# Attention plus experts on one core: a value tile kept twice, paired value products, expert outputs gathered in sorted order

## The chip, the cores and the metric

The kernel runs on one core of a Trainium2 chip. The metric is the device time of that core in microseconds (us). Differences of about 0.5% (6.5 us) are what a measurement of this kernel can tell from none.

## The reference

The input is x, 8 batches of 512 tokens with 256 channels, all float32. Layer norm, causal attention with 16 heads of 16 channels (rotary embedding on queries and keys), output projection, residual; then layer norm, a router that picks 2 of 8 experts for each token, a gated expert, and a residual again:

```
q, k, v = heads(norm(x) @ W.T + b);  q, k = rope(q), rope(k)
attn = softmax(where(causal, q @ k.T / 4, -inf));  x = x + heads_back(attn @ v) @ Wo.T + bo
logits = norm(x) @ router_w + router_b;  top 2 experts per token, probs = softmax(top 2 logits)
# each expert takes cap = int(1.2 * 2 * 512 / 8) = 153 rows of each batch, 8 * 153 = 1224 rows in all
h = rows @ w_c_fc + b_c_fc;  g = rows @ w_gate + b_gate        # 256 -> 1024
o = silu(h * g) @ w_c_proj + b_c_proj                          # 1024 -> 256
x = x + probs[0] * o[expert 0, pos 0] + probs[1] * o[expert 1, pos 1]
```

## The kernel before

Every engine has a program of its own, written out by hand; semaphores join them. There is no planner: the order of the work is the order in the code.

**Attention phase.** body(b) is one batch on each engine; it has 4 groups g of 4 heads, and each group has 8 slots u. A slot scores one block of 128 queries for two heads (pass 1, line 438, its row maxima taken by VectorE at line 823) and one block of 128 keys for two heads of the group two steps back (pass 2, lines 450 and 456, its exponentials taken by ScalarE at lines 599 and 607 into the tile probs). Between the slots TensorE does "pieces" for neighbouring batches, by the table PIECES: M transposes the row maxima (line 486), A the attention outputs of a finished group, X the normalised rows, Q and V are projections, T and O the output projection, H, L, R and F the router. free_banks makes TensorE wait, before slot u, for the maxima of slot u-2 (red_done) and the exponentials of slot u-2. The piece M in slot 0 waits for all eight maxima of the group before it. Batches 2 to 6 are one hardware loop (Fori) on each of the five engines; 0, 1, 7 and 8 are written out.

The value path: VectorE adds the bias to the value projection (line 804) into v_next, in slots (2, 5) and (3, 6) of the batch before. In slot (2, 1), with all products of the batch before done, it copies v_next (line 828) into v_sb, whose heads are padded from 16 to 32 columns, the padding holding ones. The product pv (line 467) has the values as its weights, 32 columns wide, one head at each multiple of 32 output rows, and the probabilities as the moving operand: for key block j it is 4 heads in two passes, 8 records of 512 - 128j columns. pv for j = 0, 1, 2 stands in slots 3, 5, 7, and j = 3 in slot 1 of the next group. probs holds two key blocks, so the exponentials of block j wait for the products of block j-2. Afterwards ScalarE copies the whole bank of sums (line 623) in slot 2, and piece A transposes it in slot 3.

**Expert phase.** Each expert has three blocks n of 384, 384 and 456 rows, and each block has 8 chunks hc of 128 hidden channels. For a chunk TensorE makes the fc and the gate products (line 77) in two PSUM banks each; ScalarE adds a bias to fc (line 1389), VectorE multiplies (gated, line 1484), ScalarE applies silu (line 1378), VectorE rounds to ah (line 1437), and GpSimd subtracts to al (line 1520); in the last expert VectorE does that from chunk (1, 1) on (line 1446). The output projection of a block (10 tiles of up to 128 rows per expert, 24 products each) stands after chunk 2 of the next block; VectorE adds the bias (tiles_out, line 1471) and SP stores the tile (line 1239). TensorE's gate product of chunk u needs the gated product of chunk u-2, and a projection tile needs the tile two before it put out. GpSimd also splits the weights of the next expert.

**The end.** Each token needs two rows of the expert outputs. GpSimd gathers them by indirect DMA (line 1573), 128 rows each, 8 per batch and 64 in all, in the order of the router's choices, so that a batch's rows can be those of the last expert. A batch is gathered when the last expert's tiles that hold its rows are stored. VectorE multiplies and adds (combine, line 1456, 8 per batch) to the rows loaded back into y by ScalarE's queue (line 1409), and that queue stores the result (line 1417). The loads and all sums come after the last projection.

```
            def combine(b):
                dve.wait_ge(gathered[b % len(got)], 16 * NB * (b // len(got) + 1))
                dve.wait_ge(ld_y[b % 4], 16 * (b // 4 + 1))
```

## Time and profile before

| | |
|---|---|
| runs | 1305.95, 1298.87, 1300.56 us; median 1300.56 |
| the profiled execution | 1304.85 us, of which the profile's span is 1303.0 us |
| busy in the span | TensorE 91%, VectorE 56%, ScalarE 37%, GpSimd 53% |
| TensorE busy, attention, 150 to 250 us | 94.8% |
| TensorE busy, experts, 800 to 1000 us | 99.7% |
| last 53 us | TensorE 9.6 us busy, GpSimd 34.6, VectorE 28.1 |
| chain that ended last | TensorE 48% of the span, GpSimd 2%, DMA and VectorE under 1% |
| mean granted clock of TensorE | 0.96 of full speed |

The time of an execution is its span and about 2 us around it. A "busy" matmul is a pipelined one, so busy shares near 95% still hide small losses; the starts of the instructions tell more. The attention phase ends near 560 us, the experts run to 1259 us, and what follows is gathering and adding.

### The profile page before, as it was taken

What the parts mean: (1) busy time and instruction counts of PE and PEld (TensorE: products, weight loads), DVE (VectorE), ACT (ScalarE), POOL (GpSimd) and SP (SyncE); (2) the same over time, 40 slices, a digit from 0 to 9 for tenths busy, and PEclk for the clock granted to TensorE, in tenths of its full rate; (3) what the DMA queues carried; (4) which work ended last, traced back from release to release, by engine and by line L of the source; (5) the groups of instructions that cost most, each with busy time, mean ns of one, the idle gap of its engine ahead of it and who ended that gap; (6) DMA issues with size and microseconds to landing.
All of it is one profiled execution on the core that took longest, in us unless ns stands there. A gap on an engine that the chain in (4) does not pass through costs nothing.

```text
span 1303.0 us, 25602 instructions
## 1 busy us (share of the span) xinstructions
PE 1181.2 (91%) x8264; PEld 1007.5 (77%) x8264; DVE 733.7 (56%) x1512; ACT 482.5 (37%) x988; POOL 696.3 (53%) x984
## 2 busy tenths in 40 slices
PE   3699999999999999878999999999999999999950
PEld 3466666665656576578899999999999999999950
DVE  5777787878787877755343333343433333333554
ACT  2155454545454545533333323333222333322310
POOL 4334335353535343577567655576655666742675
PEclk9699999999999999979999999999999999999985
DMA  4876745454545454442221122221111312101366
GB/s 132 213 243 178 228 115 161 113 160 113 160 113 160 113 145 113 143 136 86 74 66 58 57 75 75 74 82 57 66 63 66 109 58 66 57 29 37 102 207 235
DMA packets 83101, 147.86 MB, mean 113 GB/s; under 512 B 9647, under 2 KB 60728, under 8 KB 78910
## 3 DMA queue, kind: packets, MB, share of 16 engines
q1 hardware_dynamic: 65344, 111.37, 29.8%
q0 software_dynamic: 7936, 26.60, 6.0%
q10 hardware_dynamic: 9728, 8.67, 2.1%
q8 instruction: 56, 0.92, 0.3%
q14 instruction: 37, 0.30, 0.1%
HBM read 93.05 MB, written 53.61 MB: 113 GB/s over the span
## 4 chain that ended last, share of the span: by engine, by line
PE 48%; POOL 2%; issue 1%; DVE 0%; DMA 0%; POOLq 0%; ACT 0%; DVEq 0%
PE ps L77 47%; PE ps L1293 1%; POOL wf_hi L1573 1%; POOL wg_hi L1573 1%; POOL wp_lo L1573 0%; DVE raw L1456 0%; DMA wg_hi<-slot_outputs,slot_all 0%; DMA slot_outputs<-o_sb 0%; POOLq L1601 0%; DVE al L1446 0%; DVE xl L1361 0%; POOL wg_lo L1573 0%; DVE ah L1437 0%; ACT fc L1389 0%; POOLq L1573 0%
## 5 line engine op out<-in xcount | busy, mean ns | idle before, releaser
L1520 POOL TENSOR_TENSOR al<-hid,ah 128x384 fp32r<-128x384 f32 (+1 forms) x176 | 187.4, 1065 | 234.4 <-DVE ah L1437 234.4
L1389 ACT ACTIVATE fc<-ps,b_fc 128x384 f32<-128x384 f32 (+1 forms) x192 | 115.6, 602 | 453.2 <-PE ps L77 453.2
L1484 DVE SCALAR_TENSOR_TENSOR gated<-ps,b_gate,fc 128x384 f32<-128x384 f32 (+1 forms) x192 | 123.4, 643 | 238.8 <-PE ps L77 223.2
L823 DVE TENSOR_REDUCE mx<-ps 128x2 f32<-128x256 f32 (+3 forms) x256 | 206.1, 819 | 34.2 <-PE ps L438 31.6
L438 PE MATMUL ps<-kst,qst 65*128 65x256 f32 (+2 forms) x512 | 149.5, 375 | 10.7 <-DMA kst<-qk_parts 10.7
L607 ACT ACTIVATE probs<-ps 128x512 f32<-128x512 f32 (+1 forms) x256 | 122.9, 538 | 60.0 <-PE ps L456 59.5
L1471 DVE TENSOR_TENSOR o_sb<-ps,b_proj 128x256 f32<-128x256 f32 x80 | 33.9, 424 | 175.8 <-PE ps L77 175.8
L599 ACT ACTIVATE probs<-ps 128x256 f32<-128x256 f32 (+1 forms) x128 | 62.6, 490 | 144.3 <-PE ps L450 144.0
L964 POOL TENSOR_TENSOR rope_c<-qk_b,rope_table 128x512 f32<-128x512 f32 x32 | 43.5, 1358 | 118.4 <-ACT qk_b L635 118.3
L77 PE MATMUL ps<-xh,wg_hi 128*128 128x384 f32 (+1 forms) x384 | 103.7, 351 | 0.0
L77 PE MATMUL ps<-xh,wg_lo 128*128 128x384 f32 (+1 forms) x384 | 103.4, 351 | 0.0
L77 PE MATMUL ps<-xl,wg_hi 128*128 128x384 f32 (+1 forms) x384 | 103.4, 350 | 0.0
L1378 ACT ACTIVATE hid<-gated 128x384 f32<-128x384 f32 (+1 forms) x192 | 102.8, 535 | 1.3 <-DVE gated L1484 1.3
L467 PE MATMUL ps<-probs,v_sb 128*32 128x512 f32 (+3 forms) x1024 | 95.5, 444 | 7.5 <-DVE v_sb L828 7.5
L77 PE MATMUL ps<-wp_hi,ah 128*128 128x256 f32 (+1 forms) x640 | 89.4, 282 | 2.8 <-DVE al L1446 2.8
L77 PE MATMUL ps<-xh,wf 128*128 128x384 f32 (+1 forms) x384 | 89.1, 354 | 0.6 <-issue 0.5
L438 PEld LDWEIGHTS ps<-kst,qst 65*128 65x128 f32 x512 | 80.5, 198 | 11.1 <-DMA kst<-qk_parts 10.9
L77 PE MATMUL ps<-wp_hi,al 128*128 128x256 f32 (+1 forms) x640 | 89.0, 281 | 0.0
L1437 DVE CAST ah<-hid 128x384 fp32r<-128x384 f32 (+1 forms) x192 | 88.3, 460 | 0.8 <-ACT hid L1378 0.8
L77 PE MATMUL ps<-wp_lo,ah 128*128 128x256 f32 (+1 forms) x640 | 88.6, 281 | 0.0
L77 PEld LDWEIGHTS ps<-wp_hi,ah 128*128 128x128 f32 (+1 forms) x640 | 83.0, 185 | 3.5 <-issue 3.2
L993 POOL DMA_INDIRECT slot_tokens<-hn,put_at x64 | 63.8, 997 | 37.6 <-DVE put_at L777 21.3
(181 smaller groups left out, 2491.7 us busy)
## 6 DMA issues: line engine op xcount, KB each, us to landing
qk_parts<-hilo SPq DMA_DIRECT2D x32, 512.0 KB, 2.8
qst<-qk_parts SPq DMA_DIRECT2D x64, 256.0 KB, 4.8
kst<-qk_parts SPq DMA_DIRECT2D x64, 256.0 KB, 5.3
slot_tokens<-zeros POOLq DMA_DIRECT2D x12, 816.0 KB, 6.3
rows<-slot_tokens SPq DMA_DIRECT2D x24, 384.0 KB, 3.4
slot_outputs<-o_sb SPq DMA_DIRECT2D x72, 128.0 KB, 1.7
raw<-in_wf SPq DMA_DIRECT2D x8, 1024.0 KB, 5.4
raw<-in_wg SPq DMA_DIRECT2D x8, 1024.0 KB, 7.9
```

The costliest lines, as they stand in the source:

```text
L77: last = nc.tensor.matmul(out, w, x, start=(i == 0), stop=(i == len(terms) - 1))
L438: last = mm(bank, qst[0:MROW, g, h, bass.ts(i, P)], kst[0:MROW, g, h, 0:width], start=False, stop=True, skip_group_check=True)
L467: last = mm(pvb[32 * h:32 * h + 32, P * j:T], v_sb[:, j, GH * g + h, :], probs[:, j % 2, h, P * j:T], start=(j == 0), stop=(j == TT - 1))
L599: A(probs[:, j % 2, 2 * pr:2 * pr + 2, P * j:T], in_pairs(banks2(u)[0])[:, :, P * j - q0:T - q0], ACT.Exp, scale=float(DH) ** -0.5).then_i ...
L607: A(probs[:, j % 2, 2 * pr + hh, P * j:T], ps[:, banks2(u)[hh], P * j - q0:T - q0], ACT.Exp, scale=float(DH) ** -0.5).then_inc(exp_done, 1)
L823: V.reduce_max(mx[:, g % 2, 2 * pr:2 * pr + 2, i], both[:, :, 0:P * (i + 1)], AXX)\
L993: G.indirect_dma_start(out=rt["tok"], out_offset=bass.IndirectOffsetOnAxis(ap=put_at[:, n:n + 1], axis=0), in_=hn[:, n // K, :], in_offset ...
L1378: A(hid[:, hc % 2, 0:width], gated[:, hc % 2, 0:width], ACT.Silu).then_inc(hid_done, 1)
L1389: A(fc[:, hc % 2, 0:width], ps[:, FC + hc % 2, 0:width], ACT.Identity, bias=b_fc[:, e, hc:hc + 1]).then_inc(fc_out, 1)
L1437: V.tensor_copy(ah[:, (8 * n + hc) % RING, 0:width], hid[:, hc % 2, 0:width]).then_inc(ah_done, 1)
L1484: V.scalar_tensor_tensor(gated[:, hc % 2, 0:width], ps[:, GATE + hc % 2, 0:width], b_gate[:, e, hc:hc + 1], fc[:, hc % 2, 0:width], ALU.ad ...
L1520: G.tensor_tensor(al[:, at, 0:width], hid[:, hc % 2, 0:width], ah[:, at, 0:width].bitcast(F32), ALU.subtract).then_inc(al_done, 1)
```

## The change

- v_sb is two tiles, one for even and one for odd batches, with 17 columns per head; the bias add of the value projection writes it directly. v_next, the copy in slot (2, 1) and its semaphore are gone. The weights of pv are 17 columns wide, still at multiples of 32 output rows. The fill with ones moves from before the last value add of the opening to a place behind the small constants.
- probs is four tiles, one for each key block. pv for j = 0 and 1 both stand in slot 5, and for j = 2 and 3 in slot 1 of the next group. The exponentials of block j wait for the products of the same block of the group before.
- The loop over batches 2 to 6 is written out on all five engines.
- At the first chunk of the last expert VectorE sorts each token's two rows (11 small operations): the lower one always lies in an expert before the last. GpSimd gathers the lower rows of all batches (32 gathers) during the last expert, then the higher ones (32), batch by batch as they are stored. The higher rows use four buffers, the lower ones eight.
- The sums are half as long (4 operations) and 10 of the 16 stand between output tiles of the last two experts; y is loaded by ScalarE's queue from chunks 3 to 6 of the last expert on, and the first two stores follow in its last block.
- VectorE does all 24 subtractions of the last expert.

```
-        v_next = sb("v_next", [P, TT, C])
-        v_sb = sb("v_sb", [P, TT, HEADS, 2 * DH])
+        v_sb = sb("v_sb", [P, 2, TT, HEADS, DH + 1])
-        probs = sb("probs", [P, 2, GH, T])
+        probs = [sb(f"probs{j}", [P, GH, T - P * j]) for j in range(TT)]
...
-                    last = mm(pvb[32 * h:32 * h + 32, P * j:T], v_sb[:, j, GH * g + h, :], probs[:, j % 2, h, P * j:T],
+                    last = mm(pvb[32 * h:32 * h + DH + 1, P * j:T], v_sb[:, bt % 2, j, GH * g + h, :], probs[j][:, h, :],
...
-                        if u in (3, 5, 7) and (not isinstance(b, int) or 0 <= s - 2 <= 31):
-                            pv(s - 2, b - (g < 2), (g - 2) % 4, (u - 3) // 2)
+                        if u == 5 and (not isinstance(b, int) or 0 <= s - 2 <= 31):
+                            pv(s - 2, b - (g < 2), (g - 2) % 4, 0)
+                            pv(s - 2, b - (g < 2), (g - 2) % 4, 1)
                         if u == 1 and (not isinstance(b, int) or 0 <= s - 3 <= 31):
+                            pv(s - 3, b - (g < 3), (g - 3) % 4, 2)
                             pv(s - 3, b - (g < 3), (g - 3) % 4, 3)
...
-            with pe.Fori(2, 7) as b:
+            for b in range(2, 7):
                 body(b)
...
-                        wait(act, pv_done, 4 * t + j - 1)
+                        wait(act, pv_done, 4 * t + j - 3)
...
-                if (g, u) == (2, 1) and there(b, 0, 7):
-                    wait(dve, v_out, 2 * (b + 1))
-                    wait(dve, pv_done, 16 * b)
-                    V.tensor_copy(v_sb[:, :, :, 0:DH],
-                                  v_next[:].rearrange("p t (h r) -> p t h r", h=HEADS)).then_inc(v_moved, 1)
...
+        LOAD_Y_AT = ((0, 3), (0, 4), (0, 5), (0, 6))
+        STORE_Y_AT = ((2, 6), (2, 7))
+        COMBINE_AT = {
+            (LAST - 1, 2, 2): ((0, 0),), (LAST - 1, 2, 3): ((1, 0),),
+            (LAST, 0, 1): ((2, 0),), (LAST, 0, 2): ((3, 0),),
+            (LAST, 1, 1): ((0, 1),), (LAST, 1, 2): ((1, 1),),
+            (LAST, 2, 0): ((2, 1),), (LAST, 2, 1): ((3, 1),), (LAST, 2, 2): ((4, 0),), (LAST, 2, 3): ((5, 0),),
+        }
+        COMBINE_LAST = ((4, 1), (6, 0), (5, 1), (7, 0), (6, 1), (7, 1))
...
+            def combine(b, k):
+
+                if k == 0:
+                    dve.wait_ge(ld_y[b % len(y)], 16 * (b // len(y) + 1))
+                    dve.wait_ge(got_low[b], 16 * TT)
+                else:
+                    dve.wait_ge(low_sum, b + 1)
+                    dve.wait_ge(got_high[b], 16 * TT)
...
             def tiles_out(e, half, n, par):
...
                 for k, size in tiles(n):
+                    for b, kind in COMBINE_AT.get((e, n, k), ()) if isinstance(e, int) else ():
+                        combine(b, kind)
...
+            pool.wait_ge(gate_done, 24 * LAST)
+            pool.wait_ge(sorted_rows, 1)
+            for i in range(OB):
+                pool.wait_ge(st_o[i], 16 * NTE // OB * (LAST - 1))
+            for k in range(2):
+                for b in range(BATCH):
+                    gather(b, k)
```

The keys of COMBINE_AT are (expert, block, tile), its values (batch, 0 for the lower row or 1 for the higher), and the sum stands before that tile is put out.

## Rows read from the trace of the kernel before

**Rows 1.** Waits of TensorE, 60 to 560 us: total us, times, longest us.

```profile
PE ps L467 <- DVE v_sb L828: 7.5, 6, 1.3
PE ps L419 <- DVE mx L823: 6.1, 7, 1.0
```

**Rows 2.** Instructions that write v_sb: duration ns min/median/max, first and last start.

```profile
L828 DVE COPY v_sb<-v_next x8: 678/2528/2534, 70.6 to 507.2; 128x1024 f32<-128x1024 f32 x8
```

**Rows 3.** Timeline around the copy in slot (2, 1): start us, us, instruction [idle before].

```profile
258.37 1.06 PE L467 MATMUL ps<-probs,v_sb 128*32 128x512 f32 x8 [1.27 <-DVE v_sb L828]
...
260.25 1.28 DVE L823 TENSOR_REDUCE mx<-ps 128x2 f32<-128x512 f32 x2
...
261.07 0.28 PE L419 MATMUL ps<-causal_bf,ident_bf 128*128 128x128 bf16 x2 [1.04 <-DVE mx L823]
```

**Rows 4.** Timeline of TensorE, 300 to 345 us: slots with and without a value product.

```profile
306.51 1.07 PE L467 MATMUL ps<-probs,v_sb 128*32 128x512 f32 x8
307.51 0.66 PE L473 MATMUL ps<-consts_sb,pv_sb 128*128 128x128 f32 x4
...
313.14 0.40 PE L450 MATMUL ps<-qst,kst 66*128 66x256 f32 x2
313.38 0.63 PE L77 MATMUL ps<-xnT_hi,wq_hi 128*128 128x512 f32 x2
...
315.46 0.40 PE L450 MATMUL ps<-qst,kst 66*128 66x256 f32 x2
315.79 0.64 PE L467 MATMUL ps<-probs,v_sb 128*32 128x256 f32 x8
316.36 0.28 PE L429 MATMUL ps<-later_bf,ident_bf 128*128 128x128 bf16 x2
```

**Rows 5.** Timeline, the last maxima of a group and the piece M behind them.

```profile
284.05 2.36 DVE L823 TENSOR_REDUCE mx<-ps 128x2 f32<-128x1024 f32 x2
286.63 0.27 PE L486 MATMUL ps<-consts_sb,mx 128*16 128x128 f32 x1
335.51 0.27 PE L486 MATMUL ps<-consts_sb,mx 128*16 128x128 f32 x1 [0.45 <-DVE mx L823]
```

**Rows 6.** Timeline of VectorE in the opening, 0 to 60 us.

```profile
21.02 0.01 DVE L845 LOAD_MASK_SELECT rope_s<-qk_b  x1 [2.69 <-ACT qk_b L635]
...
36.80 1.76 DVE L909 MEMSET v_sb<- 128x2048 f32 x1 [0.38 <-issue]
```

**Rows 7.** Chain that ended last, its stores and landings: start us, us, what.

```profile
1254.42 2.39 DMA slot_outputs<-o_sb
...
1293.36 2.75 DMA wg_hi<-slot_outputs,slot_all
```

**Rows 8.** Line 1573, gathers of two batches: duration ns, first and last start us.

```profile
L1573 POOL DMA_INDIRECT wf_lo<-slot_outputs,slot_all x8: 994/998/1438, 1239.6 to 1249.3; - x8
...
L1573 POOL DMA_INDIRECT wp_lo<-slot_outputs,slot_all x8: 994/1144/1456, 1261.0 to 1271.5; - x8
```

**Rows 9.** Timeline of the end: the last eight sums.

```profile
1296.13 3.38 DVE L1456 SCALAR_TENSOR_TENSOR raw<-wg_hi,prob_all,raw 128x256 f32<-128x256 f32 x8 [5.76 <-DMA wg_hi<-slot_outputs,slot_all]
```

**Rows 10.** Timeline at chunks 3 to 5 of the last expert's first block.

```profile
1177.67 0.42 DVE L1471 TENSOR_TENSOR o_sb<-ps,b_proj 72x256 f32<-72x256 f32 x1 [2.40 <-PE ps L77]
...
1179.94 0.48 ACT L1358 ACTIVATE xh<-ps 128x384 fp32r<-128x384 f32 x1
...
1180.10 0.62 DVE L1484 SCALAR_TENSOR_TENSOR gated<-ps,b_gate,fc 128x384 f32<-128x384 f32 x1 [2.01 <-PE ps L77]
...
1183.40 0.51 PE L77 MATMUL ps<-xh,wg_hi 128*128 128x384 f32 x2
```

**Rows 11.** Line 1409, the eight loads of y: issue to landing.

```profile
DMA to landing us min/median/max: 3.9/6.5/8.9
```

**Rows 12.** Busy by stretch: length, PE, PEld, DVE, ACT, POOL, PEclk, DMA share, GB/s.

```profile
1243.50:1246.60 3.10, 0.30 (x2) 0.00 (x1) 2.57 (x5) 0.79 (x2) 2.44 (x2) 0.96 0.44 127
1246.60:1250.00 3.40, 3.37 (x17) 3.40 (x18) 0.00 (x0) 0.00 (x0) 2.71 (x3) 0.53 1.01 348
```

More of the change, by code:

```diff
@@ L580, in _ @@
             body(1)
-            with pe.Fori(2, 7) as b:
+            for b in range(2, 7):
                 body(b)
@@ L688, in _ @@
             body(1)
-            with act.Fori(2, 7) as b:
+            for b in range(2, 7):
                 body(b)
@@ L899, in _ @@
             chain(V.memset(base[:], float(E * EROWS)))
+            chain(V.memset(v_sb[:], 1.0))
             dve.wait_ge(ld_w, 16 * 10)
@@ L908, in _ @@
             first_lo(3)
-            chain(V.memset(v_sb[:], 1.0))
             body_slot(chain, -1, 3, 6)
@@ L913, in _ @@
             count[0] += body(1)
-            with dve.Fori(2, 7) as b:
-                n = body(b)
-                assert n == DVE_STEPS, n
-            count[0] += 5 * DVE_STEPS
+            for b in range(2, 7):
+                count[0] += body(b)
             count[0] += body(7)
@@ L1021, in _ @@
             pool.wait_ge(st_zero, 16 * FILLS)
-            with pool.Fori(2, 7) as b:
+            for b in range(2, 7):
                 body(b)
@@ new lines, in combine @@
+            def combine(b, k):
[5 more added lines that the diff above has]
+                    dve.wait_ge(got_high[b], 16 * TT)
+                src = got_late[b % len(got_late)] if k else got[b]
+                for t in range(TT):
+                    col = b * TT + t
+                    ins = V.scalar_tensor_tensor(y[b % len(y)][:, t, :], src[:, t, :], share[:, k, col:col + 1],
+                                                 y[b % len(y)][:, t, :], ALU.mult, ALU.add)
+                ins.then_inc((low_sum, summed)[k], 1)
@@ L1505, in _ @@
             tiles_out(LAST, LAST // 2, 2, 1)
-            for b in range(BATCH):
-                combine(b)
+            for b, kind in COMBINE_LAST:
+                combine(b, kind)
         @block.gpsimd
@@ L1524, in body @@
                 e = 2 * half + par
-                for n in range(3 if real(e + 1) else 1):
+                if not real(e + 1):
+                    hid_lo(e, 0, -1)
+                    return
+                for n in range(3):
                     for hc in range(HK):
@@ L1560, in body, with stored @@
                         late_slots("pool", e, 8 * n + hc)
-            def stored(q):
-                pool.wait_ge(st_o[q % OB], 16 * (NTE // OB * LAST + q // OB + 1))
-            def gather(b):
-                buf = b % len(got)
-                if b >= len(got):
-                    pool.wait_ge(summed, b - len(got) + 1)
-                there_now = LAST * EROWS + (b + 1) * CAP
-                for n in range(NB):
-                    G.indirect_dma_start(
-                        out=got[buf][:, n, :], out_offset=None, in_=rt["o"][0:there_now],
-                        in_offset=bass.IndirectOffsetOnAxis(ap=rt["slot"][:, b * NB + n:b * NB + n + 1], axis=0),
-                        bounds_check=there_now - 1, oob_is_err=False).then_inc(gathered[buf], 16)
-            late_slots("pool", 0, -1)
-            experts(pool, body)
-            hid_lo(LAST, 1, -1)
-            pool.wait_ge(gate_done, 24 * LAST)
-            pool.wait_ge(proj_done, NTE * LAST)
-            for i in range(OB):
-                pool.wait_ge(st_o[i], 16 * NTE // OB * LAST)
-            rows_out = 0
-            for b in range(BATCH):
+            def stored(e, b):
                 for q in range(NTE):
```

130 lines of the change are left out of this document (86 added, 44 removed).

## The prediction

> **What bounds the kernel now.** I read the busy time by stretch first, then TensorE's waits, then the timeline at each wait, then the chain that ended last. The reader is to see three regimes. In attention and in the experts TensorE runs nearly without a gap, so a wait of TensorE there is time lost one for one, and work taken off another engine counts only if TensorE waited for it. After the last projection GpSimd's gathers set the end.
>
> In attention two waits stand out [rows 1]: 7.5 us for the copy into v_sb and 6.1 us at line 419 for maxima. One place makes both: the copy takes 2.53 us in six of the eight batches and 0.68 in the first and last [rows 2], the product behind it starts 1.27 us late, and VectorE, still behind, makes the mask of slot 4 wait 1.04 us more [rows 3].
>
> **The copy goes.** Before, the product began at 258.37 after an idle 1.27, so slot 3 had ended at 257.10. After, that product stands in slot 5; piece A, about 0.5 us, brings TensorE to slot 4 at 257.6. VectorE's two maxima began at 260.25 [rows 3]; without 2.53 us of copy they begin at 257.72, and the first of the two (0.69 or so of 1.28) is there at about 258.45. So a backlog that the moved product used to cover is now bare: TensorE starts slot 4 at 258.45 and not at 261.07, 2.62 us sooner, of which 1.06 is the product that comes later. That is 1.56 us per batch, 9.4 us in six. The upper bound is both waits whole, 2.31 x 6 = 13.9; the lower the first wait alone, 7.5. The bias add keeps its 128x512 elements and only writes rows of 17; it costs the same, bounded by the copy's own slow form: 16 adds up to 1.8 us slower, none of it on TensorE's path unless it delays the maxima of slots 6 and 7.
>
> **Paired value products.** A slot's last product is followed by the next work after 0.24 us (313.14 to 313.38) but by a value product after 0.33 (315.46 to 315.79): entering costs 0.09 [rows 4]. The products take 0.57 us at 256 columns (315.79 to 316.36) and 1.00 at 512 (306.51 to 307.51), so 256 columns are 0.43 and 0.14 is left over. If both are paid once per visit, a pair saves 0.23 us; 2 pairs x 32 groups = 64 make 14.7 us. The bounds are 0 (the 0.14 and 0.09 belong to each key block) and 14.7. I take the upper end: the only difference between the two neighbours in [rows 4] is the change of kind of work. By the Trainium skill (TensorEngine Tiling (Array Packing), Key Properties) a change of tiling mode drains the engine while a change of tile does not, which would make the price one per visit and the sum the same as mine; with the lower bound it would be 14.7 more. The trace agrees as far as the 0.09 goes.
>
> **What the pairing uncovers.** The product for j = 2 leaves slot 7 and stands behind piece M of slot 0. It cost 316.36 - 315.46 - 0.24 = 0.66 us there [rows 4], so TensorE comes to M 0.66 us sooner; M needs the last maxima. Those end at 286.41 (284.05 + 2.36) for an M at 286.63 that did not wait, and one M in four waits 0.45 already [rows 5]. VectorE does not get there earlier, for its maxima of slots 6 and 7 follow scores that come no sooner. So the M with 0.22 us of slack now waits 0.44, the one that waits gets all 0.66 more; three in four of the first kind give 0.50 on average, times 32 = 16.0 us. Bounds: 0 (VectorE, freed elsewhere, keeps ahead) and 0.66 x 32 = 21. The pairing thus gains 14.7 and loses 16.0: I enter +1.3. The move of j = 0 from slot 3 to 5 uncovers nothing else but what is counted above; the exponentials' waits all get looser.
>
> **Loop written out, fill moved.** No wait of TensorE in the loop region stands at the loop's end; none is counted, with 2 us either way. The fill (1.76 us, somewhat longer for 2176 elements) moves into VectorE's idle 2.69 us before 21.02 [rows 6]: nothing.
>
> **The end.** Before, the last tile but two landed at 1254.42 + 2.39 = 1256.81 [rows 7], and two batches of eight gathers each and more were still to issue. After, the lower rows are gathered during the last expert. Its first chunk lies four output tiles of 2.82 us (0.42 + 2.40) and two chunks of some 2 us ahead of 1177.67 [rows 10], near 1162; sorted by 1164, the 32 low gathers at 1.39 each are done near 1209, and the higher ones of batches 0 to 4 follow as they are stored, before 1250 (estimates). What is left behind 1256.81 is batches 5, 6 and 7: 12 gathers. Their pace is 1.39 us each amid the experts' work (9.7 / 7) and 1.50 amid sums and loads (10.5 / 7) [rows 8]; I take 1.45. The last begins at 1256.81 + 11 x 1.45 = 1272.8, lands 2.75 us later [rows 7] at 1275.5, its four sums take half of 3.38 [rows 9], 1277.2, and the store and what follows is 1303.0 - 1299.51 = 3.5 us: the span ends at 1280.7, 22.3 us sooner.
>
> The eight gathers of 1239.6 to 1249.3 ran beside the last chunks of the experts at 1.39 us apiece [rows 8], so I let VectorE's casts cost the low gathers nothing. The Trainium skill (SBUF — State Buffer, SBUF: two separate sides) says that a DMA issued from GpSimd is starved of descriptors while VectorE runs a copy or cast in its two-port mode, which speaks against gathering during the last expert; by that rule the sum would be that of rival 4, and the trace's 1.39 does not bear it out.
>
> **The new wait.** The sum of batch 1's lower rows stands before the last output tile of expert 6, and waits for the second load of y. ScalarE issues that load at chunk 4, behind the fc, silu and xh of chunk 3, which TensorE makes only after the projection: 1179.94 + 0.48 = 1180.42 [rows 10]. It lands after 3.9 us at best, median 6.5 with four loads at once [rows 11]; it goes out alone, so 3.9: 1184.3. Then four sums (1.69), the output tile (0.42) and the gated product of chunk 3 (0.62) [rows 9, 10]: 1187.1. Queued behind it on VectorE is every gated product, and TensorE's gate product of chunk 5, at 1183.40 [rows 10], needs the one of chunk 3: it stands for 3.7 us. After an idle of about 3 us the granted clock was 0.53 for the next 3.4 us, the lower of the two levels (1.2 of 2.4 GHz) for nearly all of it [rows 12]; that costs 3.4 x 0.47 = 1.6 us more. Together 5.3; bounds 0 (the load lands before the projection's end: excluded by its place, so 3) and 5 more for the slowest landing. The eleven sorting operations, about 2.7 us at 0.2 apiece and waits, and the eight subtractions moved to VectorE lie beside the projection that follows chunk 2; if they ran late, the first output tile would be late and add up to 1 us. The other sums, 1.7 us, fit between output tiles 2.8 us apart.
>
> **Sum.** -9.4 (copy), +1.3 (pairing), 0 (loop, fill), -22.3 (end), +5.3 (new wait) = -25.1 us. Against the profiled execution's own 1304.85 that is 1279.8; it lies 4.3 above the median of the runs, so against 1300.56 the forecast is 1275.5.
>
> **Rivals.**
> 1. *All at the good end.* No new M waits, pairs save whole, both waits at the copy go: -13.9 - 14.7 - 22.3 + 3 = -47.9, 1252.7. For it: most M do not wait today. Against: its maxima end 0.22 us before M [rows 5]. Chance 0.15.
> 2. *The uncovered waits win.* Pairs save nothing, M waits 21 us, the copy gives 7.5, the load lands late (10 in place of 5.3): -7.5 + 21 - 22.3 + 10 = +1.2, so 1302, no difference. Full strength is unlikely; half of it, near 1288, is not. Chance 0.12, of which half within 0.5%.
> 3. *Slower: 17-column weights lose the parallel heads.* The eight records of 256 columns take 0.57 us, while two of a full-width product take 0.24 (313.14 to 313.38), so eight in a row would take 0.96 [rows 4]. It is 0.39 more at 256 columns, for the mean 320 columns 0.49, and 128 visits make +62 us: 1275.5 + 62 = 1338. It decides as soon as the four heads no longer run side by side; half of the effect is enough for slower. No row shows a weight of under 32 columns at such an offset. By the Trainium skill (TensorE: Matmul & The Clock Gate, What picks the tile position) the start partition of the output picks the column tile, which speaks against it. Chance 0.05.
> 4. *The gathers starve during the last expert.* If each of the 32 low gathers lost one cast, about 0.5 us, they would end 16 us later, near 1224, and the high ones of batches 0 and 1 near 1236, some 5 us past the output tiles that their sums stand before: TensorE stands up to 7 us more, 1282.5 (estimates, from the times above). Chance 0.06.
>
> The forecast has 0.62. The range takes in its bounds (copy 7.5 to 13.9, pairing -14.7 to +21 of which both ends are rare, new wait 3 to 10) and the better half of rival 2: 1257 to 1291. Rival 3 and parts of 1 and 2 are left out. Faster by over 0.5%: 0.62 + 0.15 + 0.06 + 0.06 = 0.89; within 0.5% (what a measurement of this kernel can tell from no change): 0.06; slower: 0.05.
>
> **What would show it.** In the profile after: no wait for v_sb, the wait of line 419 in slot (2, 4) below 1 us; M (line 486) waiting about 0.5 us in nearly every group; value products in pairs that take 0.23 us less than before; gathers from about 40 us after expert 7's start no longer dense at the end, the last one 12 gathers after the second last-block tile landed; one gap of 3 to 5 us in TensorE about 24 us into the last expert, waiting at line 77 for gated, followed by half clock; and about 21 us from TensorE's last product to the end of the span in place of 43. It is wrong if attention shortens by more than 20 us or not at all, or if TensorE's gap is missing.

## The result, and the profile after

The changed kernel takes 1292.11 us (median of 6 runs), the kernel before beside it 1302.67. The ratio on record is 0.9927 with a 95% interval of 0.9897 to 0.9956, which is 9.5 us faster; the two medians are 10.6 us apart. The forecast was 25.1 us faster, 1275.5 with a range of 1257 to 1291; the measured time lies 1.1 us above that range. The profiled execution took 1290.96 us for a span of 1288.9.

The time at the end came as forecast, more or less: the span now ends 25.0 us after TensorE's last product (1263.9) and not 43.4. But that last product ends 4.4 us *later* than before (1259.6). So nothing was won in the 1200 us ahead of it, where the forecast had 8.1 us in attention. Attention is not shorter at all, which the forecast named as a sign that it is wrong: the first piece M of batch 7 starts at 495.3 us and started at 494.6.

First TensorE's waits from 60 to 560 us in the kernel after, total us, times and longest; they answer to [rows 1].

```profile
PE ps L418 <- DVE mx L826: 11.1, 7, 2.0
PE ps L485 <- DVE mx L826: 9.6, 14, 1.7
PE ps L77 <- DVE attn L792: 8.1, 10, 1.2
```

The wait for v_sb is gone. But line 418 (419 before) waits 11.1 us for maxima and not 6.1, and two waits have grown, of the transpose M (line 485, 486 before) and of a Q or V piece that needs its bank back from attn. In the kernel before they were:

```profile
PE ps L486 <- DVE mx L823: 4.3, 7, 1.7
PE ps L77 <- DVE attn L791: 1.0, 6, 0.2
```

The three places in one middle batch, from the timeline (start us, us, instruction, idle before):

```profile
241.68 0.74 PE L77 MATMUL ps<-xnT_hi,wk_hi 128*128 128x512 f32 x2 [1.19 <-DVE attn L792]
...
258.40 0.28 PE L418 MATMUL ps<-causal_bf,ident_bf 128*128 128x128 bf16 x2 [2.01 <-DVE mx L826]
...
268.41 0.27 PE L485 MATMUL ps<-consts_sb,mx 128*16 128x128 f32 x1 [0.82 <-DVE mx L826]
```

What holds the maxima up at slot (2, 4), once the copy is gone? The timeline there, GpSimd and VectorE, one batch later:

```profile
318.27 2.84 POOL L979 TENSOR_TENSOR xr<-xr,bo_all 128x1024 f32<-128x1024 f32 x1
...
319.13 0.20 DVE L771 TENSOR_REDUCE pos<-posm 128x8 f32<-128x64 f32 x1
...
319.37 1.78 DVE L772 TENSOR_SCALAR over<-pos 128x8 f32<-128x8 f32 x1
...
321.18 0.23 DVE L774 TENSOR_SCALAR pos<-pos,base 128x8 f32<-128x8 f32 x1
...
322.72 1.28 DVE L826 TENSOR_REDUCE mx<-ps 128x2 f32<-128x512 f32 x2
```

An operation on eight numbers per partition takes 1.78 us. It ends at 321.15, and GpSimd's add of the bias onto xr ends at 321.11. This operation took 0.17 us before, where it stood behind the copy; the copy then took 2.53 us in six batches and 0.68 in two [rows 2]. The same batch of the kernel before:

```profile
319.85 2.83 POOL L983 TENSOR_TENSOR xr<-xr,bo_all 128x1024 f32<-128x1024 f32 x1
...
320.70 2.53 DVE L828 COPY v_sb<-v_next 128x1024 f32<-128x1024 f32 x1
```

The copy ended at 323.23, 0.55 us after GpSimd's add (322.68), which is less than the 0.68 us that it needs alone. So the suspicion is that the copy's 2.53 us were mostly that same wait, and that it has only passed to the next in line.

Behind the wait the clock falls. Two stretches of the kernel after, before and behind the 2.01 us of one batch (length, PE, PEld, DVE, ACT, POOL, PEclk, DMA share, GB/s):

```profile
188.80:192.20 3.40, 1.42 (x12) 1.14 (x11) 3.23 (x9) 1.71 (x5) 1.58 (x2) 1.00 0.67 198
192.20:195.60 3.40, 3.37 (x17) 3.29 (x18) 2.02 (x4) 0.60 (x1) 3.07 (x4) 0.55 0.22 77
```

TensorE was busy 1.42 of 3.4 us; then the granted clock was 0.55, nearly all of it the lower level, 1.2 of 2.4 GHz. In the kernel before there was no such stretch between 73 and 552 us; here three of the five middle batches have one. The wait alone does not tell which: in the next batch TensorE was busy 1.39 us of the 3.4 from 255.0 on, and the clock stayed at 1.00.

The products of two key blocks, as pairs, with what follows each (they answer to [rows 4]):

```profile
308.85 0.40 PE L449 MATMUL ps<-qst,kst 66*128 66x256 f32 x2
309.18 1.70 PE L466 MATMUL ps<-probs,v_sb 128*17 128x512 f32 x16
310.81 0.20 PE L533 MATMUL ps<-onehot_bf,tri_bf 128*128 128x64 bf16 x1
```

A pair of 512 and 384 columns takes 1.63 us; alone, in the run moved_and_early below, the two take 0.98 and 0.77:

```profile
235.05 1.05 PE L466 MATMUL ps<-probs,v_sb 128*17 128x512 f32 x8
236.03 0.66 PE L472 MATMUL ps<-consts_sb,pv_sb 128*128 128x128 f32 x4
...
239.98 0.84 PE L466 MATMUL ps<-probs,v_sb 128*17 128x384 f32 x8
240.75 0.20 PE L533 MATMUL ps<-onehot_bf,tri_bf 128*128 128x64 bf16 x1
```

That saves 0.12 us, and the second entry of 0.09 is saved too. The forecast had 0.23 per pair; that stands.

In the last expert, at the place of [rows 10], the new wait is there: VectorE's second early sum, and TensorE's gate product behind it.

```profile
1184.49 1.67 DVE L1506 SCALAR_TENSOR_TENSOR raw<-wf_hi,share,raw 128x256 f32<-128x256 f32 x4 [7.97 <-DMA raw<-x_rows]
...
1187.07 0.62 PE L77 MATMUL ps<-xh,wg_hi 128*128 128x384 f32 x2 [2.27 <-DVE gated L1534]
```

And the end, which answers to [rows 7 to 9]: the output tile that batch 5's gathers wait for, GpSimd's last twelve gathers (first, third and last) and VectorE's sums. The third gather runs beside two sums in a row; the last sum waits 4.28 us for the last gather.

```profile
1258.35 0.42 DVE L1521 TENSOR_TENSOR o_sb<-ps,b_proj 128x256 f32<-128x256 f32 x1 [0.82 <-PE ps L77]
...
1262.46 1.19 POOL L1637 DMA_INDIRECT wp_hi<-slot_outputs,row_of  x1 [13.80 <-issue]
...
1264.33 1.66 DVE L1506 SCALAR_TENSOR_TENSOR raw<-wp_hi,share,raw 128x256 f32<-128x256 f32 x4
...
1265.26 3.18 POOL L1637 DMA_INDIRECT wp_hi<-slot_outputs,row_of  x1 [0.31 <-issue]
...
1265.91 1.66 DVE L1506 SCALAR_TENSOR_TENSOR raw<-wg_lo,share,raw 128x256 f32<-128x256 f32 x4
...
1279.77 1.00 POOL L1637 DMA_INDIRECT wp_lo<-slot_outputs,row_of  x1 [0.30 <-issue]
...
1283.66 1.67 DVE L1506 SCALAR_TENSOR_TENSOR raw<-wp_lo,share,raw 128x256 f32<-128x256 f32 x4 [4.28 <-DMA wp_lo<-slot_outputs,row_of]
```

### The profile page after: what moved, and what is told of

Its sections match the earlier page's. It is cut to its first block, busy times and chain, and to the rows that moved or that the text cites. A ratio compares the mean times of both kernels' runs of the same rounds, so it can differ in the third digit from the quotient of the medians.

```text
span 1288.9 us, 24008 instructions
## 1 busy us (share of the span) xinstructions
PE 1175.9 (91%) x8264; PEld 1014.6 (79%) x8264; DVE 729.0 (57%) x1523; ACT 490.3 (38%) x988; POOL 689.1 (53%) x976
## 4 chain that ended last, share of the span: by engine, by line
PE 47%; issue 2%; POOL 1%; DMA 1%; DVE 1%; ACT 0%; POOLq 0%; DVEq 0%
PE ps L77 46%; PE ps L1309 1%; POOL wp_lo L1637 1%; POOL wp_hi L1637 0%; DMA raw<-x_rows 0%; DMA wp_lo<-slot_outputs,row_of 0%; DVE raw L1506 0%; DVE gated L1534 0%; DVE xl L1377 0%; ACT hid L1394 0%; POOLq L1657 0%; DVEq L1657 0%; DVE ah L1465 0%; DVE o_sb L1521 0%; DVE al L1474 0%
## 5 line engine op out<-in xcount | busy, mean ns | idle before, releaser
L1572 POOL TENSOR_TENSOR al<-hid,ah 128x384 fp32r<-128x384 f32 (+1 forms) x168 | 179.3, 1067 | 214.5 <-DVE ah L1465 214.5
L466 PE MATMUL ps<-probs,v_sb 128*17 128x512 f32 (+3 forms) x1024 | 82.5, 440 | 0.0
L77 PEld LDWEIGHTS ps<-wp_hi,al 128*128 128x128 f32 (+1 forms) x640 | 81.3, 185 | 0.0
```

What stands on the lines that cost most here:

```text
L77: last = nc.tensor.matmul(out, w, x, start=(i == 0), stop=(i == len(terms) - 1))
L466: last = mm(pvb[32 * h:32 * h + DH + 1, P * j:T], v_sb[:, bt % 2, j, GH * g + h, :], probs[j][:, h, :], start=(j == 0), stop=(j == TT - 1))
L1572: G.tensor_tensor(al[:, at, 0:width], hid[:, hc % 2, 0:width], ah[:, at, 0:width].bitcast(F32), ALU.subtract).then_inc(al_done, 1)
```

## The experiments

Sixteen kernels ran in four groups, each group on a chip of its own and with the kernel before beside it. The kernel before took 1355.7 us on the first of these chips, and 1302.4, 1302.4 and 1302.7 on the other three. A time is only compared within those three; of the first group the ratios and single rows count.

### First group: undo one part, or do one alone

**unpaired**, the kernel after with

```diff
-  if u == 5: pv(s - 2, ..., 0); pv(s - 2, ..., 1)
-  if u == 1: pv(s - 3, ..., 2); pv(s - 3, ..., 3)
+  if u in (3, 5, 7): pv(s - 2, ..., (u - 3) // 2)
+  if u == 1: pv(s - 3, ..., 3)
```

> The kernel after, with the value products back one key block at a time in slots 3, 5, 7 and 1 (the four probability tiles, the doubled value tile and the new end stay). Theory A, the pairing is a net loss in the loop, because the transpose of the maxima and the Q, K and V pieces now stand where products used to cover VectorE's maxima and attention (waits in 60-560: 9.6 + 8.1 us after against 4.3 + 1.0 before, 12.4 us) and this costs more than what the pairs save at their entry: this kernel is 3 to 8 us faster than the changed one, 1284 to 1289, with the transpose waiting about 4 us in total again. Theory B, the pairing pays its full 14.7 us and the loop lost its gain elsewhere: this kernel is slower than the changed one by 2 us or more, 1294 or later. Theory C, the two cancel as the prediction had it (+1.3): 1290 to 1293.

**end_only**, the kernel before with everything of the diff from `LAST = E - 1` on.

> The kernel before with only the new end (sorted entries, low gathers beside the last expert, combines from the experts on); attention is as before. Theory A, the whole measured gain is the end and the attention part of the change gives nothing: the time is within 2 us of the changed kernel's, 1289 to 1294, with the last gathers starting within 1 us of the changed kernel's distance from the last product. Theory B, the attention part gives the 8 us of the prediction and the end less than it seems: 1296 or later. Theory C, the attention part costs time: 1287 or faster.

**no_bias_add**, the kernel after with

```diff
-  G.tensor_tensor(xr[:], xr[:], bo_all[:]..., ALU.add)
+  G.tensor_tensor(xr[:, 0, 0:8], xr[:, 0, 0:8], bo_all[:, 0:8], ALU.add)
```

This kernel leaves the output projection's bias out of all but 8 columns of one tile, so its output is not the reference's; it is there for its timeline.

> The kernel after with GpSimd's bias add on the residual tile cut from 128x1024 to 128x8 elements, so the output projection's bias is left out of all but 8 columns. Theory A, VectorE's first shared-memory-to-shared-memory operation of that slot waits for GpSimd's 2.8-us add, whether it is the copy (before, 2.53 us) or the 128x8 tensor_scalar (after, 1.78 us): that tensor_scalar falls to 0.17 us, the masks of slot (2,4) wait under 0.6 us instead of 2.0, the 3.4-us stretches at half clock behind them in the loop go, and the kernel is 8 to 18 us faster than the changed one, 1274 to 1284. Theory B, the tensor_scalar is long for a reason of its own (its place, a semaphore): it stays above 1.5 us and the time within 2 us of the changed kernel's.

**pair_only**, the kernel before with `probs` as four tiles and the pairing's lines.

> The kernel before with only the pairing (a probability tile for each key block, products of blocks 0 and 1 in slot 5 and of 2 and 3 in slot 1; 32-column value tile, copy, loop and end as before). Theory A, pairing is a net loss: 3 to 8 us slower than before, 1305 to 1311. Theory B, it pays 14.7 us less uncovered waits of about 5: 8 us or more faster, 1295 or less. Theory C, the prediction's sum of -14.7 and +16.0: 1302 to 1305.

Measured, against a before of 1355.7 us: unpaired 1326.7, ratio 0.9773 (0.9730 to 0.9816); end_only 1350.5, 0.9968 (0.9937 to 0.9999); no_bias_add 1324.1, 0.9772 (0.9727 to 0.9816); pair_only 1379.9, 1.0183 (1.0137 to 1.0230).

As times these decide little, for on this chip something else takes part. ScalarE and VectorE of end_only, and TensorE, in a batch whose third interval between transposes was 23.5 us instead of 16.1:

```profile
274.95 0.76 DVE L823 TENSOR_REDUCE mx<-ps 128x2 f32<-128x256 f32 x2 [4.48 <-remote]
...
275.07 1.08 ACT L607 ACTIVATE probs<-ps 128x512 f32<-128x512 f32 x2 [5.35 <-remote]
...
276.34 3.78 PE L511 MATMUL ps<-wo,attnT 128*128 128x256 f32 x8 [4.75 <-ACT negmax L614]
```

Three engines stand still together, while GpSimd issues its scatters. None of this is in a trace of the other chips. It also seems to have taken most of the new end's gain: from 1203 to 1228 us of end_only TensorE stood 20 times "for issue", 15.8 us in all, beside the early gathers, and in the kernel after it never did. So no theory on a time is settled here; the direction of pair_only (slower) is.

One reading does not depend on the chip. Line 772 in no_bias_add, count, duration ns min/median/max, first and last start, and the wait at the masks of line 418 from 60 to 560 us:

```profile
L772 DVE TENSOR_SCALAR over<-pos x8: 171/172/1257, 187.0 to 600.1; 128x8 f32<-128x8 f32 x8
```

```profile
PE ps L418 <- DVE mx L826: 1.8, 5, 0.4
```

Against 171/1778/1780 ns and 11.1 us in the kernel after. Without GpSimd's long add the small operation takes 0.17 us in six batches (1.26 and 0.69 in the last two, behind the middle ones) and most of TensorE's wait goes: theory A of that run in both of these rows. Its time, 8 to 18 us under the kernel after, can't be judged, for the kernel after did not run on this chip. The second interval between transposes is 16.1 to 16.2 us there, against 17.7 to 19.2.

### Second group: the sum of the parts

> The changed kernel once more, beside the runs of this call. It is the yardstick for the runs that undo a part of it: in the first call, where the kernel before took 1355.7 us and not 1302.7, the engines stood still together for 4 to 5 us at a time while GpSimd's indirect scatters ran (ACT from 269.7 to 275.1, VectorE from 270.5 to 274.9, TensorE from 271.6 to 276.3 in the run with the new end alone). Theory A, a property of that chip: here the ratio to before is again 0.99 and the loop's batches take 65 to 66.5 us. Theory B, a property of the kernels of that call: it doesn't come back here either, but the ratio stays 0.99 and the first call's ratios stand as they are. If before takes over 1340 us here too, the ratio of this run tells what the change is worth on such a chip: 0.975 to 0.985 by the runs unpaired and no_bias_add (0.977 each), if those two edits are worth little.

**loop_only**, the kernel before with

```diff
-  with pe.Fori(2, 7) as b:
+  for b in range(2, 7):
       body(b)
```

and the same on the other four engines.

> The kernel before with only the five middle batches written out in place of the register loop. Theory A, the prediction's zero: within 2 us of before. Theory B, register waits and the branches of 0.22 us on each engine cost something in the rolled loop: 1 to 5 us faster. Theory C, more instructions to fetch (q8 56 to 69 packets): 1 to 5 us slower.

**value_only**: the head of unpaired (values straight into the doubled tile, no copy, 17 columns, four tiles of probabilities, loop written out) with the old end.

> The kernel before with the value path of the change (values straight into the doubled padded tile, no copy, 17 columns), the loop written out, four probability tiles, but the value products unpaired and the old end. Theory A, the copy's 1.85 us above its own 0.68 was a wait for GpSimd's bias add that now falls on the next operation, so only the copy's own time and the 1.27-us wait of the product behind it go: 1 to 4 us faster than before, with the 128x8 tensor_scalar that followed the copy at 1 to 2 us. Theory B, the prediction's -9.4: 8 to 12 us faster, that tensor_scalar at 0.17 us.

> The changed kernel with the value products unpaired, as in the first call, now beside the changed kernel itself. Theory A, the pairing is a net loss of 3 to 8 us: this run is so much faster than after_again. Theory B, pairing and unpairing are worth the same: within 2 us of after_again. Theory C, the pairing gains: 3 us or more slower than after_again.

Measured, against a before of 1302.4: after_again 1292.0, ratio 0.9927 (0.9910 to 0.9945); loop_only 1297.5, 0.9960 (0.9945 to 0.9975); value_only 1296.9, 0.9950 (0.9933 to 0.9968); unpaired_again 1281.6, 0.9830 (0.9807 to 0.9852).

The result comes back to the fourth digit, and it now falls into parts that were measured: the loop written out -4.9 us; the value path 1296.9 - 1297.5 = -0.6; the new end 1281.6 - 1296.9 = -15.3; the pairing 1292.0 - 1281.6 = +10.4. The sum is -10.4. The intervals of these runs are about 2 to 3 us either way, so the value path can't be told from nothing, and the pairing is 10.4 by the medians and 12.6 by the ratios.

For where in attention they fall, these are the times from one transpose M to the next (worked out from the starts of line 485 or 486) for the five middle batches. Each batch is four groups. The last two columns are of batches 2 to 5: the last interval of batch 6 is shorter in every kernel, 12.7 to 12.9 us.

| kernel | M0 to M1 | M1 to M2 | M2 to M3 | M3 to M0 | batch |
|---|---|---|---|---|---|
| before | 15.5 | 18.1 to 18.2 | 16.1 | 15.2 | 65.0 |
| loop_only | 15.5 | 17.6 to 17.9 | 16.0 | 14.9 | 64.1 to 64.4 |
| value_only | 15.5 | 16.8 to 18.3 | 16.0 | 14.9 | 63.1 to 64.7 |
| unpaired_again | 15.5 | 16.8 to 18.3 | 16.0 | 14.9 | 63.1 to 64.7 |
| after_again | 16.7 | 17.7 to 19.2 | 16.3 | 14.4 | 65.0 to 66.6 |
| pair_early | 16.4 | 18.6 to 20.0 | 15.9 | 14.3 | 65.1 to 66.5 |
| paired_moved | 16.7 | 16.1 to 16.4 | 16.2 to 17.8 | 14.5 | 63.4 to 65.3 |
| before_moved | 15.5 | 16.3 to 16.4 | 16.1 | 15.2 | 63.1 |
| add_moved | 15.5 | 15.1 to 15.5 | 16.0 | 14.9 | 61.5 to 61.8 |
| late_pair | 15.8 | 15.5 to 15.7 | 16.4 | 15.0 | 62.7 to 62.9 |
| moved_and_early | 15.5 | 15.2 | 16.0 | 14.9 | 61.5 |

loop_only is theory B: 0.6 to 0.9 us per batch, in the intervals after M1 and M3, 3.8 us over the five batches of the profiled executions; by which instruction, no run tells. value_only misses theory A's "1 to 4 us" because the loop's 4.9 are in it, and misses theory B's 8 to 12 by more; its small tensor_scalar took 1.77 us, as A had it. The column M1 to M2 shows the rest: removing the copy took 0.8 us out of a batch (17.6 to 16.8), but in two of the five batches, and in four of five in unpaired_again, the wait of 1.3 us that is left at slot (2, 4) is now followed by a stretch at half clock: the interval is 18.3 us at a mean granted clock of 0.91, against 16.8 at 1.00, and no better than before.

### Third group: move the add, load early, halve the pairing

**add_moved**, unpaired with nothing left out and

```diff
   # SP
-  if (g, u) == (1, 4) and there(b, 1, 8):   # load of xr
+  if (g, u) == (0, 1) and there(b, 1, 8):
   # GpSimd
-  if (g, u) == (2, 1) and there(b, 1, 8):
+  if (g, u) == (0, 6) and there(b, 1, 8):
       wait(pool, ld_xr, 16 * b)
+      wait(pool, xn_done, min(b + 2, BATCH))
```

> The changed kernel with the value products unpaired (1281.6 us beside a before of 1302.4) and with the load of the residual tile issued at slot (0,1) and GpSimd's 2.8-us bias add at slot (0,6), behind VectorE's normalisation of the next batch, where VectorE has nothing to do from shared memory to shared memory for 4 us. Nothing is left out. Theory A, VectorE's first such operation of slot (2,1) waits for that add wherever it stands there: the 128x8 tensor_scalar falls from 1.78 to 0.17 us, the interval between the second and third transposes of the maxima from 16.75 or 18.3 us to 15.0 to 15.4 in all the middle batches (no stretch at half clock behind the wait of slot (2,4)), and the kernel is 10 to 20 us faster than unpaired, ratio to before 0.968 to 0.975. Theory B, the wait goes elsewhere a second time (the tensor_tensors of slots (0,6) to (1,2) get longer, or TensorE waits at slot (2,4) as before): within 4 us of unpaired, ratio 0.980 to 0.986.

**load_early**, unpaired with

```diff
-  LOAD_Y_AT = ((0, 3), (0, 4), (0, 5), (0, 6))
+  LOAD_Y_AT = ((0, 1), (0, 2), (0, 3), (0, 4))
```

> The changed kernel with the value products unpaired and the loads of the residual rows y two chunks earlier (chunks 1 to 4 of the last expert's first block in place of 3 to 6). Theory A, the 8.15-us wait of VectorE's second early combine for its load is what TensorE's 2.4-us wait for the gated tile in the last expert comes from: that wait and the 0.4 us behind it go, and the kernel is 2 to 4 us faster than unpaired, ratio to before 0.980 to 0.981. Theory B, the end is set by the gathers behind the last rows of the products and these start by a store that follows the last product, so the same 2 to 4 us show there too; if they don't (the end within 1 us of unpaired's) something other than TensorE sets the end.

**pair_early**, the kernel after with blocks 2 and 3 back in slots 7 and 1.

> The changed kernel with key blocks 0 and 1 paired in slot 5, and blocks 2 and 3 back in slots 7 and 1, so half of the pairing. Theory A, the two halves cost by their uncovered waits: this half the waits of the Q and V pieces behind slot 4 for VectorE's attention (8.1 against 1.4 us) and the other half those of the transpose (9.6 against 2.9); each about half of the 10.3 us between 1281.6 and 1292.0, this kernel at 1285 to 1289. Theory B, all of the loss is the transpose's, which every group's chain of maxima runs through: 1279 to 1283. Theory C, all of it is this half: 1290 to 1294.

**moved_and_early**, add_moved and load_early together.

> Both: value products unpaired, GpSimd's bias add at slot (0,6), loads of y two chunks earlier; nothing left out. Theory A, the two gains add: 12 to 23 us under unpaired, ratio to before 0.966 to 0.973, faster than both kernels of the case. Theory B, the port theory is wrong and only the loads pay: 0.979 to 0.982.

Measured, against a before of 1302.4: add_moved 1269.7, ratio 0.9750 (0.9737 to 0.9763); load_early 1279.8, 0.9824 (0.9809 to 0.9840); pair_early 1291.2, 0.9917 (0.9902 to 0.9931); moved_and_early 1264.9, 0.9725 (0.9709 to 0.9741).

Moving one 2.8-us add of GpSimd and the load that it needs, with every operation kept, is worth 11.9 us on the unpaired kernel: theory A, at the edge of its ratio. That it is the add and not the load shows in no_bias_add, where the load stayed, the add was cut, and the interval M1 to M2 (16.1 to 16.2) is that of paired_moved. Line 770, the small tensor_scalar of this kernel, took 0.17 us in all five middle batches, the interval M1 to M2 fell to 15.1 to 15.5 us, and from 160 to 460 us TensorE was busy 293.2 us at a granted clock of 1.00. The small operation is long once more in this trace, behind the middle batches, and again it ends with an instruction of GpSimd, this time another one, from the weights of the experts (534.64 after 534.62):

```profile
530.09 4.53 POOL L1085 TENSOR_TENSOR wp_lo<-raw,wp_hi 128x2048 fp32r<-128x2048 f32 x1 [3.36 <-DVE wp_hi L1081]
...
531.61 3.03 DVE L770 TENSOR_SCALAR over<-pos 128x8 f32<-128x8 f32 x1
```

The stretch from 160 to 460 us of moved_and_early, and of the kernel after behind it:

```profile
160.00:460.00 300.00, 294.03 (x2365) 203.45 (x2367) 243.31 (x543) 154.56 (x327) 143.60 (x235) 1.00 0.54 144
```

```profile
160.00:460.00 300.00, 272.05 (x2198) 195.57 (x2194) 236.11 (x511) 148.72 (x309) 132.37 (x212) 0.98 0.50 133
```

load_early gained 1.9 us, just under what A expected, and its interval overlaps that of unpaired_again; but TensorE's wait for the gated tile is gone from its trace. On top of add_moved the same edit gave 4.8 us, and there the two intervals still touch. In the trace of the kernel after the wait was 2.7 us (2.27 and the 0.41 behind it); what its going is worth in time is known no closer than that.

pair_early is theory C: half of the pairing costs 9.6 of the 10.4 us. Its waits from 60 to 560 us:

```profile
PE ps L418 <- DVE mx L827: 13.4, 7, 2.4
PE ps L77 <- DVE attn L793: 7.8, 9, 1.2
```

With the product of block 0 gone from slot 3, TensorE reaches slot 4 earlier, and there both the late maxima and attn are still to come; in unpaired_again these two waits are 6.5 and 1.4 us. All five middle batches of pair_early have a stretch at half clock.

### Fourth group: does the pairing lose by itself, and was the copy the add?

**paired_moved** is the kernel after and **before_moved** the kernel before, each with the two moves of add_moved. **sum_order** is moved_and_early with

```diff
-  COMBINE_LAST = ((4, 1), (6, 0), (5, 1), (7, 0), (6, 1), (7, 1))
+  COMBINE_LAST = ((4, 1), (5, 1), (6, 0), (7, 0), (6, 1), (7, 1))
```

and **late_pair** is moved_and_early with blocks 2 and 3 paired in slot 1.

> The changed kernel as it is, paired, with only the load of the residual tile at slot (0,1) and GpSimd's bias add at (0,6). Theory A, the pairing's 10.3 us come for the greater part from what it uncovers at slot (2,4): TensorE comes there earlier, waits 2.0 us in place of 1.3 for maxima that are late because of GpSimd's add, and falls to half clock; with the add away the loss shrinks to the prediction's order, this kernel at 1271 to 1275 against 1269.7 unpaired. Theory B, the uncovered waits of the transpose and of the Q and V pieces cost the 10 us by themselves: 1277 to 1281. Theory C, without that wait the pairing pays: under 1268.

> The kernel before with the load of the residual tile at slot (0,1) and GpSimd's bias add at (0,6), nothing else; the copy of the values stays, also the rolled loop. Theory A, the copy's 2.53 us are 0.68 of its own and 1.85 of waiting for the add: all its executions take about 0.68 us, the wait of the product behind it (1.3 us) goes, and this edit alone gives the better part of what was forecast for removing the copy: 8 to 14 us faster than before, 1288 to 1294. Theory B, the copy is long by itself there: it stays at 2.5 us and the time within 3 us of before.

> moved_and_early with two sums of the end in another order: (4,1), (5,1), (6,0), (7,0) in place of (4,1), (6,0), (5,1), (7,0), so that after the last product VectorE no longer does two sums of 1.67 us each in a row beside GpSimd's gathers. Theory A, the one gather of 3.5 us (1.0 elsewhere) was held up until both sums were done: it falls to about 1.9 us, and the end comes 1 to 2 us earlier, 1263 to 1264. Theory B, the long gather has a reason of its own (its first rows, the store before it): it stays at 3.5 us and the time within 0.5 us of 1264.9.

> moved_and_early with only key blocks 2 and 3 paired, in slot 1, blocks 0 and 1 in slots 3 and 5; the half of the pairing that cost 0.8 us in the presence of the wait at slot (2,4). Theory A, the transpose's uncovered wait and the saved entries cancel: 1263 to 1267. Theory B, with slot (2,4) free of the wait the pair's saving shows: 1258 to 1262. Theory C, the transpose's wait is the whole cost now that nothing else waits: 1268 to 1272.

Measured, against a before of 1302.7: paired_moved 1281.3, ratio 0.9837 (0.9818 to 0.9856); before_moved 1292.4, 0.9917 (0.9904 to 0.9930); sum_order 1264.0, 0.9707 (0.9691 to 0.9722); late_pair 1272.6, 0.9765 (0.9748 to 0.9782).

before_moved shows what the copy was:

```profile
L828 DVE COPY v_sb<-v_next x8: 676/678/693, 69.6 to 496.2; 128x1024 f32<-128x1024 f32 x8
```

0.68 us in all eight batches, and 10.3 us off the kernel, theory A. Moving one load and one add in the old kernel is worth as much as the whole change.

paired_moved is 11.6 us slower than add_moved, theory B, a little above its range: the pairing loses by itself, with one stretch at half clock in the five batches against none. Its waits from 160 to 460 us, and those of add_moved behind them:

```profile
PE ps L77 <- DVE attn L792: 7.2, 10, 1.2
PE ps L485 <- DVE mx L826: 6.5, 10, 1.1
PE ps L472 <- DVE xnT_lo L799: 2.4, 5, 0.5
...
PE ps L418 <- DVE mx L826: 2.0, 5, 0.4
```

```profile
PE ps L485 <- DVE xnT_lo L797: 2.4, 5, 0.5
PE ps L485 <- DVE mx L824: 1.7, 5, 0.5
```

late_pair is 7.7 us slower than moved_and_early, theory C and a little past it. So each half costs 8 to 10 us alone (the early one measured with the add in its old place, the late one with it moved) and both together 10 to 12. A reading of this, which no run tests: once TensorE waits for VectorE in a group, being earlier elsewhere in it adds little.

sum_order's time is in theory A's range but within its interval of moved_and_early. The gather of 3.48 us took 2.51, and another now took 2.08; with the sums of VectorE beside them:

```profile
1238.13 2.51 POOL L1636 DMA_INDIRECT wp_hi<-slot_outputs,row_of  x1 [0.30 <-issue]
...
1247.71 2.08 POOL L1636 DMA_INDIRECT wp_lo<-slot_outputs,row_of  x1 [0.31 <-issue]
```

```profile
1238.10 1.66 DVE L1505 SCALAR_TENSOR_TENSOR raw<-wp_hi,share,raw 128x256 f32<-128x256 f32 x4
...
1245.66 3.25 DVE L1505 SCALAR_TENSOR_TENSOR raw<-wg_lo,share,raw 128x256 f32<-128x256 f32 x8
```

Both gathers end 0.88 us after the sums end (1240.64 after 1239.76, 1249.79 after 1248.91). The long gather of moved_and_early ended as far behind its sums (1239.58 after 1238.70), and so did that of the kernel after (1268.44 after 1267.57). So a long gather goes on until VectorE's sums are done, as theory A had it. But most gathers beside such sums took only 1.0 to 1.3 us, in the same traces; which one is held stays open.

sum_order is the fastest of all that ran, with moved_and_early beside it: 38.7 us under the kernel before.

## Why the prediction failed, step by step

**The copy (-9.4 forecast, -0.6 measured, and not to be told from 0).** The step was "without 2.53 us of copy they begin at 257.72": the whole duration was taken as work that leaves with the instruction. Only 0.68 us of it was. The evidence was in the forecast's own row: the same instruction with 678 ns at the least and 2528 in the middle [rows 2]. Two durations for one shape mean a wait inside the instruction, and the question was what ran beside it in the six long ones. The maxima did begin 2.5 us sooner by the clock (322.72 for 325.25), but 1.5 us of that was the group standing earlier (its transpose at 315.79 for 317.3); measured from the transposes the gain was 0.8 us per batch, and a stretch at half clock (1.5 us) took more than that back in two to four of five. What took the wait's place is the 128x8 operation, 1.78 us for 0.17. The Trainium skill (SBUF — State Buffer, Who interferes with whom) says that VectorE's copy and tensor_scalar in their two-port modes take a port pair shared with GpSimd, which whoever comes first holds for the whole instruction, and that on this chip tensor_reduce never takes part. This case agrees: beside the add of 318.27 to 321.11 the reduce took 0.20 us and the tensor_scalar 1.78. The forecast read that page for its DMAs only.

**The pairing (+1.3 forecast, +10.4 measured).** The gain was sized right: 0.12 + 0.09 = 0.21 us for a pair of 512 and 384 columns against 0.23, some 13 us in 64 pairs. The loss was not 16.0 but about 24 (10.4 and the 13 saved, an estimate). The part for the transposes held in size: late_pair alone lost 7.7 us and the 6.7 that its 32 pairs save, 14.4. It did not hold in form: M waited in 14 groups, 9.6 us in all, and not about 0.5 us in nearly every group. The step that failed is "the move of j = 0 from slot 3 to 5 uncovers nothing else". It uncovers slot 4: the piece there needs the bank that VectorE's attn must free (8.1 us of waits against 1.4 in unpaired_again), and the masks there meet the late maxima (2.01 us against 1.3).

**Loop and fill (0 forecast, -4.9 measured).** "No wait of TensorE in the loop region stands at the loop's end" was true and not the question; the 0.6 to 0.9 us per batch lie inside it. The fill cost nothing that shows, as forecast: the first transpose M starts at 52.33 us, 53.69 before.

**The end (-22.3 forecast, about -18).** The place and the count of the gathers were right. From the landing of the tile that batch 5 waits for (1258.77 + some 2.4 = 1261.2) the first of twelve began 1.3 us late, the eleven intervals took 17.3 us and not 16.0 (one gather of 3.18 us), and the last took 3.9 us from its start to its sum and not 2.75. Together 3.7 us.

**The new wait (+5.3 forecast, about +2.7).** It came where forecast, 2.27 us at the gate product and 0.41 behind it; the load issued at the forecast's 1180.42 was summed from 1184.49, against 1184.3. TensorE had come there later than reckoned (1184.80 and not 1183.40), and no half clock followed: the granted clock was 1.00 from 1183.4 to 1190.2 us, though TensorE was busy only 1.40 of the first 3.4 us.

**Rivals.** Rival 3 (heads no longer side by side) did not come: a product of 512 columns takes 0.98 us with weights of 17 columns and 1.00 with 32. Rival 4 neither: the 32 low gathers ran at 1.34 us each beside the casts. The likeliest case had 0.62; what happened is nearest rival 2, 1302 in full and "half of it, near 1288": little from the copy, and uncovered waits above the gain. It fell just outside the range because the range allowed the copy no less than its first wait, 7.5 us. A lower bound of zero was due: the wait could pass on. That it missed the range by 1.1 us only is luck: the loop's 4.9 us and the cheaper new wait (2.6 us) hid a third of what copy, pairing and end fell short (8.8, 9.1 and about 4).

## What to carry to other kernels

When the same instruction shows two durations, find what runs beside it in the long cases before pricing its removal: if the time is a wait, it goes to the next instruction that needs the same thing, and moving the partner is what pays. A filler between a producer and its consumer is worth what it covers; gathering fillers into pairs saved 0.2 us each time and uncovered more at both places it left. And ask for a bound of zero wherever a stall could only change its place.

## What the hardware showed unexpectedly

GpSimd's 128x1024 add made a VectorE tensor_scalar of 128x8 elements take 1.78 us in place of 0.17, as long as the add had still to run; the add in turn took 2.83 us at slot (2, 1) and 2.37 at slot (0, 6), where VectorE only reduced from PSUM or added with one input from there. The reduce of 128x64 beside the same add took 0.20 us, as it did without it.

A TensorE that had been busy 1.42 us of 3.4 was then granted 0.55 of its clock for 3.4 us. The same kernel was busy 1.39 us of 3.4 a batch later and kept its full clock; the waits of 1.3 us at the same slot in value_only were followed by a stretch at half clock in two batches of five, in unpaired_again in four.

Of four chips three ran the same kernel before at 1302 to 1303 us and one at 1356. On the slower one several engines stood still together for 4 to 5 us beside indirect DMAs of GpSimd, and the new end, which puts more of those beside TensorE, gained 0.3% there; on the others it gave 15 us (1.2%), by the difference of unpaired_again and value_only. No run tells what differs in that chip.

In nine profiled kernels with the new end one gather took 3.16 to 3.56 us among gathers of 1.0 to 1.3. In all nine it ended 0.87 to 0.88 us after the second of two sums of VectorE in a row.
